# Stage seams, batch-wise row writes, grouped routing and a second accumulator in a two-layer decoder kernel

## What is computed

```python
x = LN(x + spectral(x))                       # fft filter and a bit-correcting code
x = LN(x + gated(x, ctx))                     # two attentions, mixed by a gate
# first ffn: 8 experts, 512 given rows each (rows may repeat)
out_e = gelu(x[tok] @ W1[e] + b1) @ W2[e] + b2
x = LN(x + scatter_add(tok, out_e * combine[tok, e]))
x = LN(x + self_attention(rope(x), 16 heads of 16))
x = LN(x + cross_attention(x, ctx, 16 heads of 64))
# second ffn: 32 experts, top 8 of softmax(x @ gate), capacity 256 rows each
h = silu(x_e @ Wg[e]) * (x_e @ Wu[e])
x = LN(x + scatter_add(slots, (h @ Wdown[e]) * weight))
```

## Time and profile before

| what | us |
| --- | --- |
| median of three runs | 2322.5 |
| lowest and highest | 2320.73, 2326.05 |
| profiled execution | 2315.22 |
| span of its trace | 2313.3 |
| gated to first ffn, no matmul | 380 to 412.9 |
| first ffn to first row maximum of self_heads | 654 to 747.1 |
| cross_heads loop | 1200 to 1936 |
| routing | 1938 to 2050 |
| expert loop, first to last store | 2065.15 to 2283.8 |
| last norm | 2283.8 to 2313.3 |

### The profile page before, as it was taken

The page is one execution under the profiler, slowest core; times in us unless marked ns, Lnnn a source line. Parts: engine busy times, 40 slices in busy tenths (PEclk is TensorE's granted clock), DMA queues, the critical chain, the costliest instruction groups (busy, mean ns, idle before and its releaser), DMA issues. The chain is left out here.

```text
span 2313.3 us, 23934 instructions
## 1 busy us (share of the span) xinstructions
PE 1738.0 (75%) x7497; PEld 1256.8 (54%) x7497; DVE 1236.0 (53%) x2315; ACT 1020.0 (44%) x1920; POOL 1009.3 (44%) x838
## 2 busy tenths in 40 slices
...
DMA packets 88421, 138.38 MB, mean 60 GB/s; under 512 B 19728, under 2 KB 54974, under 8 KB 85480
## 3 DMA queue, kind: packets, MB, share of 16 engines
...
## 5 line engine op out<-in xcount | busy, mean ns | idle before, releaser
L1961 POOL TENSOR_TENSOR STp_lo_use<-ST_use,STp_hi_use 128x512 fp32r<-128x512 f32 x256 | 335.1, 1317 | 163.4 <-ACT ST_use L1812 158.7
L1526 POOL TENSOR_TENSOR STp_lo<-ST,STp_hi 128x512 fp32r<-128x512 f32 x192 | 257.5, 1359 | 117.3 <-ACT ST L1359 116.2
L1808 ACT ACTIVATE STp_hi_use<-bank 128x512 fp32r<-128x512 f32 x256 | 152.8, 597 | 199.2 <-PE bank L1758 196.7
L1355 ACT ACTIVATE STp_hi<-bank 128x512 fp32r<-128x512 f32 x256 | 159.6, 624 | 73.2 <-PE bank L1293 72.6
L1427 DVE TENSOR_REDUCE nmax<-bank 128x1 f32<-128x512 f32 x256 | 168.7, 681 | 34.5 <-PE bank L1282 34.1
L1871 DVE TENSOR_REDUCE nmax_use<-bank 128x1 f32<-128x512 f32 x256 | 170.6, 681 | 5.0 <-PE bank L1732 2.3
L1282 PE MATMUL bank<-rows_k,rows_q 96*128 96x512 f32 x256 | 122.6, 487 | 52.0 <-DVE nmax L1427 44.7
L1359 ACT ACTIVATE ST<-bank 128x512 f32<-128x512 f32 x256 | 161.0, 629 | 0.0
L1812 ACT ACTIVATE ST_use<-bank 128x512 f32<-128x512 f32 x256 | 151.8, 593 | 0.0
L1732 PE MATMUL bank<-ks,qs 128*128 128x512 f32 x256 | 115.9, 454 | 30.3 <-DVE nmax_use L1871 16.2
L2396 POOL DMA_INDIRECT acc_scratch<-res,sidx_all x64 | 101.8, 1591 | 54.9 <-DMA acc_scratch<-res,sidx_all 33.9
...
## 6 DMA issues: line engine op xcount, KB each, us to landing
...
```

What stands on the lines that cost most here:

```text
L1355: A.activation(STp[u % NHI][0], bk.ap, ACT.Exp)
L1526: G.tensor_tensor(STp[u % NHI][1], ST[u % NFULL], plain(STp[u % NHI][0]), ALU.subtract).then_inc(low["pool"].sem, low["pool"].inc(u))
L1808: A.activation(STp[u % NHI][0], bk.ap, ACT.Exp)
L1961: G.tensor_tensor(STp[u % NHI][1], ST[u % NFULL], plain(STp[u % NHI][0]), ALU.subtract).then_inc(low["pool"].sem, low["pool"].inc(u))
```

## The change

- **gated to mixture.** `store(k)` on SP writes the rows of batch k to `rows_scratch` and to the sums while `gated` still works on later batches. The row numbers and combine weights are loaded in `gated`; `tok_row` comes expert by expert (256 KB). The four DMAs of POOL and the two halves are gone.
- **mixture to self_heads.** `norm_sums` is no longer called here. POOL goes on without waiting for its last stores and takes no part in the barrier; the others wait for the stores of the last expert but one. The loads of the sums, statistics, roots and norms are written into `self_heads`: quarter 0 and the statistics of 1 ahead of the step loop, the rest at of_next(s, 38). Zeroing `Vone` moves from DVE to POOL, the zeroing of `rows_q` and `rows_k` goes (one `memset` of one row stays). For batch 0 q0, q1, k0, k1 and the four v results each get a bank of their own. The hop is written by head: 10 DMAs a batch instead of 4, and 4 reads a quarter instead of 9; for batch 0 ACT issues the k half of them.
- **self_heads and cross_heads.** Row tiles have 65 rows instead of 96. In `cross_heads` the takes of the second head move from r = 7 to r = 6 and the output projection and the norm's steps by 2 (one entry by 6).
- **routed.** Rows in `tokens_scratch` are 288 wide, with the 32 weights behind the row, so that a gather brings its weight along. Transposes of a batch run ahead of the logits of the one before; the eight largest are taken batch by batch. The running sum on POOL becomes 15 wide matmuls. BV is made by 16 ACT instructions a group, only for the slots, in f32r with 128 columns. The slot table is written, read back and turned for each group of eight experts, and gathers and stores wait only for their group.
- **two accumulators.** Even experts add into one array, odd ones into another that is filled with zeros by a DMA from DRAM to DRAM; a store waits for the expert before the last. The last norm loads both, and DVE adds them (4 x 128x1024).

```diff
+                if other is not None:
+                    V.wait_ge(others_in[k].sem, others_in[k][k])
+                    V.tensor_tensor(X[:, quarter[k], :], X[:, quarter[k], :], other[:, quarter[k], :], ALU.add).then_inc(added.sem, added.inc(k))
...
+        def store(k):
+
+            tiles = slice(k * TB, (k + 1) * TB)
+            SP.wait_ge(own.sem, own["s2 normed", k])
+            SP.dma_start(kit.rows_d.rearrange("(t p) d -> p t d", p=P)[:, tiles, 0:D], X[:, tiles, :]).then_inc(kit.rows_in.sem, kit.rows_in.inc(k))
+            SP.dma_start(kit.acc_d[0][0:B * S].rearrange("(t p) d -> p t d", p=P)[:, tiles, :], X[:, tiles, :]).then_inc(kit.sums_in.sem, kit.sums_in.inc(k))
+
...
         def pool():
-            G.dma_start(idx, T["idx"]).then_inc(idx_in.sem, idx_in.inc("idx"))
-            G.dma_start(rows_d[:, D:GW], T["combine"]).then_inc(combine_in.sem, combine_in.inc("combine"))
-            G.dma_start(acc_d[0:B * S].rearrange("(t p) d -> p t d", p=P), X).then_inc(acc_in.sem, acc_in.inc("acc"))
-            G.dma_start(tok_row, bass.AP(T["tok"].tensor, 0, [[0, P], [1, E0 * C0]])).then_inc(tok_in.sem, tok_in.inc("tok"))
...
+                SP.dma_start(tok_row[e % 2], bass.AP(T["tok"].tensor, e * C0, [[0, P], [1, C0]])).then_inc(tok_in[e % 2].sem, tok_in[e % 2].inc(e))
...
-        nc.all_engine_barrier()
-    norm_sums(kit, "s3")
+        for engine in (PE, A, V, SP):
+            engine.wait_ge(stored.sem, stored[E0 - 2, CT0 - 1])
+        nc.multi_engine_barrier([PE.engine, A.engine, V.engine, SP.engine])
...
+        def stack_bank(b, n, g):
+
+            return (SPARE, ROW_BANK, *OUT_BANKS)[2 * n + g] if b == 0 else SPARE
+
+        def v_bank(b, t):
+            return (*ST_BANKS, *MAX_BANKS)[t] if b == 0 else SPARE
...
+        def norm_loads(engine, quarters):
+
+            engine.wait_ge(kit.stored0.sem, kit.stored0[E0 - 1, CT0 - 1])
+            for k in quarters:
+                engine.dma_start(X[:, quarter[k], :], tiles_d[:, quarter[k], :]).then_inc(kit.quarter_in[k].sem, kit.quarter_in[k].inc("s3"))
...
+        def stack_rows(engine, b, i, n):
+
+            hs = slice(i * HS, (i + 1) * HS)
+            for k in range(2):
+                first = k * n * HD
+                engine.dma_start(plain((rows_q, rows_k)[n][2 * k * HD:2 * (k + 1) * HD, hs]), hop_d[b % 2, n, hs, first:first + 2 * HD].rearrange("h f s -> f h s")).then_inc(stacked[i].sem, stacked[i].step)
...
-            V.memset(plain(Vone), 0.0).then_inc(own.sem, own.inc("s4 V"))
-            V.wait_ge(own.sem, own["s4 V"])
...
+            average(0)
+            average(1)
+            norm(0)
...
+                if of_next(s, 38) == 0:
+                    norm(1)
+                    average(2)
+                    norm(2)
+                    average(3)
+                    norm(3)
...
-            for rows in (rows_q, rows_k):
-                m = G.memset(plain(rows[MAX_ROW:ROWS]), 0.0)
...
+            G.memset(plain(Vone), 0.0).then_inc(g_own.sem, g_own.inc("s4 V"))
...
-        OUTS = ((50, 0, 0), (58, 0, 1), (STEPS + 18, 1, 0), (STEPS + 24, 1, 1))
+        OUTS = ((50, 0, 0), (58, 0, 1), (STEPS + 24, 1, 0), (STEPS + 25, 1, 1))
...
-                for r, of, half in ((3, "q", 0), (5, "k", 0), (7, "q", 1), (7, "k", 1)):
+                for r, of, half in ((3, "q", 0), (5, "k", 0), (6, "q", 1), (6, "k", 1)):
...
+                def slot_table(g):
+                    PE.wait_ge(slots_in.sem, slots_in[g])
+                    PE.wait_ge(bank[3].free, bank[3].use(("table", g)))
+                    PE.transpose(bank[3].ap[:, 0:16], slot_rows[:, g, :], ident[0:16, 0:16]).then_inc(bank[3].full, 1)
...
                     for t in range(NT):
-                        m = PE.matmul(bank[1 + z].ap[:, 0:256], A_[z][:, t, :, :].rearrange("p e j -> p (e j)"), BV[z][:, t, :, :].rearrange("p v j -> p (v j)"), start=t == 0, stop=t == NT - 1)
+                        m = PE.matmul(bank[1 + z].ap[:, 0:P], A_[z][:, t, :, :].rearrange("p e j -> p (e j)"), BV[z][:, t, :], start=t == 0, stop=t == NT - 1)
...
-                m.then_inc(bank[3].full, 1)
+                    if g:
+                        slot_table(g - 1)
+                slot_table(3)
...
+                for g in range(4):
+                    z = g % 2
+                    A.wait_ge(hot_b.sem, hot_b[g])
+                    if g > 1:
+                        A.wait_ge(bank[1 + z].full, bank[1 + z].full_at["slots", g - 2])
+                    for t in range(NT):
+                        m = A.activation(BV[z][:, t, :], B_[z][:, t, :, :].rearrange("p e j -> p (e j)"), ACT.Copy, scale=token1[:, t:t + 1])
+                    m.then_inc(hot_v.sem, hot_v.inc(g))
...
+                for g in range(4):
+                    e8, z = slice(g * 8, g * 8 + 8), g % 2
+                    if g > 1:
+                        V.wait_ge(bank[1 + z].full, bank[1 + z].full_at["slots", g - 2])
+                        V.wait_ge(hot_v.sem, hot_v[g - 2])
+                    V.tensor_tensor(B_[z], every(lo[:, :, e8], 16), along(ramp[:, 16:32]), ALU.is_equal).then_inc(hot_b.sem, hot_b.inc(g))
+                    V.wait_ge(own.sem, own["high bits"])
+                    V.tensor_tensor(A_[z], every(hi[:, :, e8], 16), along(ramp[:, 0:16]), ALU.is_equal).then_inc(hot_a.sem, hot_a.inc(g))
+                    if g == 0:
+                        weigh()
+                    if g:
+                        agree(g - 1)
+                    if g > 1:
+                        addresses(g - 2)
+                agree(3)
+                addresses(2)
+                addresses(3)
...
-                    G.tensor_tensor(value(z, 0), B_[z], per_tile(token1), ALU.mult).then_inc(hot_v.sem, hot_v.inc(g))
...
-                SP.dma_start(tokens_d.rearrange("(t p) d -> p t d", p=P), X).then_inc(rows_in.sem, rows_in.inc("rows"))
-                SP.dma_start(acc_d[0:B * S].rearrange("(t p) d -> p t d", p=P), X).then_inc(acc_in.sem, acc_in.inc("acc"))
+                SP.dma_start(acc_d[0][0:B * S].rearrange("(t p) d -> p t d", p=P), X).then_inc(acc_in.sem, acc_in.inc("sums"))
+                SP.dma_start(acc_d[1], bass.AP(T["zeros"].tensor, 0, [[0, (B * S + CAP) * D // 4096], [1, 4096]])).then_inc(acc_in.sem, acc_in.inc("zeros"))
+                SP.dma_start(tokens_d[:, 0:D].rearrange("(t p) d -> p t d", p=P), X).then_inc(rows_in.sem, rows_in.inc("rows"))
                 for e in range(WB):
                     load(e)
+                SP.wait_ge(own.sem, own["weight"])
+                SP.dma_start(tokens_d[:, D:].rearrange("(t p) e -> p t e", p=P), weight).then_inc(rows_in.sem, rows_in.inc("weight"))
                 for g in range(4):
                     SP.wait_ge(own.sem, own["slots", g])
-                    for v in range(2):
-                        SP.dma_start(slot_d[v, g * 2048:(g + 1) * 2048].rearrange("(p j) -> p j", j=16), slots[:, g, v, :]).then_inc(slots_out.sem, slots_out.inc((g, v)))
-                SP.wait_ge(slots_out.sem, slots_out[3, 1])
-                SP.dma_start(slot_rows, slot_d.rearrange("v (r c) -> r v c", c=P)).then_inc(slots_in.sem, slots_in.inc("rows"))
+                    SP.dma_start(slot_d[g * 2048:(g + 1) * 2048].rearrange("(p j) -> p j", j=16), slots[:, g, :]).then_inc(slots_out.sem, slots_out.inc(g))
+                    SP.wait_ge(slots_out.sem, slots_out[g])
+                    SP.dma_start(slot_rows[:, g, :], slot_d[g * 2048:(g + 1) * 2048].rearrange("(r c) -> r c", c=P)).then_inc(slots_in.sem, slots_in.inc(g))
...
-                    G.wait_ge(bank[e % 2].full, bank[e % 2].full_at["rows1", e - RB])
+                    bk = bank[6 + (e - RB) % 2]
+                    G.wait_ge(bk.free, bk.free_at["down1", e - RB])
+                if e % 8 == 0:
+                    G.wait_ge(own.sem, own["gidx", e // 8])
                 for t in range(CT1):
...
-            G.wait_ge(own.sem, own["gidx"])
+            G.wait_ge(rows_in.sem, rows_in["weight"])
...
-            G.wait_ge(own.sem, own["sidx"])
+            G.wait_ge(acc_in.sem, acc_in["zeros"])
...
-                if e:
-                    G.wait_ge(stored.sem, stored[e - 1, CT1 - 1])
+                if e % 8 == 0:
+                    G.wait_ge(own.sem, own["sidx", e // 8])
+                if e > 1:
+                    G.wait_ge(stored[e % 2].sem, stored[e % 2][e - 2, CT1 - 1])
...
-                    G.indirect_dma_start(acc_d, bass.IndirectOffsetOnAxis(ap=sidx[:, n:n + 1], axis=0), res[e % 2][:, t, :], None,
-                                         compute_op=ALU.add).then_inc(stored.sem, stored.inc((e, t)))
-            G.wait_ge(stored.sem, stored[E1 - 1, CT1 - 1])
+                    G.indirect_dma_start(acc_d[e % 2], bass.IndirectOffsetOnAxis(ap=sidx[:, n:n + 1], axis=0), res[e % 2][:, t, :], None,
+                                         compute_op=ALU.add).then_inc(stored[e % 2].sem, stored[e % 2].inc((e, t)))
...
-        nc.all_engine_barrier()
-    norm_sums(kit, "s6", kit.out)
```

(1 more changed line is left out.)

454 lines of the change are left out of this document (245 added, 209 removed).

## The result

The changed kernel took **2384.8 us** (median of four runs, 2374.5 to 2393.6) against 2322.5 before: a ratio of **1.027, 95% interval 1.022 to 1.031**. It is slower, by 62 us, where the prediction had it faster by 145. The profiled execution has a span of 2373.2 against 2313.3, 59.9 more.

What follows compares the result with a forecast made beforehand. It took PE to bound dense self_heads and cross_heads, POOL the expert loop, and chains the seams. Terms -24 - 35.6 + 3 - 33 - 35.4 - 22 + 2 = -145 took 2322.5 to 2177 us, range 2138 to 2222.

Steps and rivals of the forecast that it cites:

- Rival (4): self_heads: the new start, PE standing still behind DVE's norms, keeps the granted clock low; 2387 for whole stage, chance 0.03.
- Gated to mixture: Seam from gated's last norm to mixture: gathers start at about 382 instead of 406.19; 24 us gained, range 20 to 26.
- could be late next: Start of mixture: the first expert's weights, 2 MB issued at the same time as the gathers, might be late; nothing priced.
- Mixture to self_heads: Seam from mixture's last store to the first row maximum of self_heads: 35.6 us earlier, range 28 to 40.
- xT: Start of self_heads: the normed, transposed input of the projections is ready at 675.0 instead of 701.66, 26.7 us earlier.
- hop 3, read back 5: Start of self_heads: rows of k go out in 3 us and return in 5, arriving at about 709.
- Inside self_heads: Between first and last row maximum of self_heads: extra hop issues and more pieces at a batch's turn cost 3 us.
- Cross_heads: cross_heads: earlier takes of the second head give 26 us, moved output projections 7; together 33, range 0 to 50.
- An `nmax` wait that takes over from the k wait: cross_heads, a sign of being wrong: PE's wait for maxima grows by what its wait for the second head's k lost.
- Routing: From the end of cross_heads to the first experts of routed: a shorter chain gains 35.4 us, range 26 to 40.
- Expert loop: Expert loop of routed: two accumulators cut the pitch from 6.99 to 6.5, last five experts 5; 22 us gained, range 5 to 31.
- Tail: After the last store: drain and barrier of 5.1 go, but more loads and DVE adds come; 2 us longer.

Runs made afterwards that it cites:

- b_both: Kernel before, with the maximum matmul of self_heads reading 64 rows and the score matmul 65, instead of 96: 2500.7 us, ratio 1.077.
- b_both65: Kernel before, with both the maximum and score matmuls of self_heads reading 65 rows instead of 96: 2323.5 us, ratio 1.001.
- a_pad96: Kernel after, with self_heads row tiles padded by 32 zero rows, so the maximum matmul reads 96 rows and the score matmul 97: 2188.0 us, ratio 0.942.
- a_pad_g: a_pad96 with each head group's hop issued once that group is split, and ACT waiting only for the hop whose place it takes: 2162.7 us, ratio 0.935.

## Why the prediction was wrong

**The step that failed** is one the sum does not even hold: "Row tiles have 65 rows instead of 96" was priced at nothing, without a reason, and the edits of self_heads at +3. No sentence of the prediction weighs the row count. One matmul's length would not have warned: the longest maximum matmul takes 796 ns with 96 rows and 794 with 64. The runs show that the row count changes the clock itself: 177 us between `b_both` and `b_both65`, 197 between the kernel after and `a_pad96`. The change cut rows from 96 to 65 in both matmuls' tiles, but the maximum matmul, which leaves out the row with the maxima, thereby went to 64, on the other side of the edge.

**Rival (4)** gave 2387 with the low clock for the whole stage; 2384.8 came. Its size came out, 196 by the earlier trace rows against 203.8, but by luck: it took the clock for 0.50 throughout, and the stage had 0.62 in the mean; PE was busy for 240 us more, and 36 of them came out of the time in which it had stood still. Its trigger was wrong: it blamed PE's standing still at the new start, and counted for the old clock that "PE stood still just as often there". It got a chance of 0.03, with only that trigger weighed. The trigger that counted stood in the diff.

**Seams.** Gated to mixture: 24 forecast, 17.7 came. The gather came on time, 25.7 earlier; what was mis-sized is the way from there to `GT_hi`, which the prediction left as it was and which took 8.0 us more: 5.1 for the rows to arrive and 2.9 on ACT behind the weights. Of the weights the prediction said that they "could be late next", and priced nothing for them. In the trace after, SP issued them from 385.10 and ACT could take the second half only at 400.95. Mixture itself had no term and grew by 4.9, 4.5 of them in the wait of its last store. Mixture to self_heads: 35.6 forecast, 31.7 came; xT was right within 1.1, and what lacks came behind it. The last half of k was ready sooner than forecast, 9.7 us after the first projection instead of 13, but its rows reached PE 21.0 later, where the prediction had "hop 3, read back 5": the hop's ten issues end only at 696.4. DVE's norms, which the prediction had as late as the rows, were hidden.

**Inside self_heads.** +3 was put for "four hop issues more a batch on SP (0.4 each)". There are six more, 10 instead of 4. They took 0.7 to 1.5 at the medians and up to 1.7, and they do not lie beside the loop: ACT waits for their landing before it takes the next group of the projections. The term is +20 in `a_pad96` and -0.6 in `a_pad_g`.

**Cross_heads.** 26 + 7 forecast, 43.4 came, 39 to 42 of it by the takes alone. PE did stand still for 26 us less, but that the number agrees is partly luck: at the matmul of the forecast the wait fell by 16 (47.1 to 31.1), since the maxima are late there, and 13 came at the first matmul of a step, of which the sum had nothing; others grew. An `nmax` wait that takes over from the k wait was one of the signs of being wrong that the prediction named, and two thirds of it came true. The projections gave next to nothing. What the sum had no line for is again the clock: a PE that waits less was granted 0.98 instead of 0.95, which is worth 16 us of busy time.

**Routing.** 35.4 forecast, 43.4 came: the first expert's transposes are 40.4 earlier (the prediction's own 2050.16 less 2012.5 is 37.7, not 37.4, and it took off 2 for the zero array), and its first store follows them after 12.0 us instead of 15.0. The claim that rows are "long there" when PE reaches the experts is borne out: holding the gather back until the last group costs 7.7, or 16 by the ratios.

**Expert loop.** 22 forecast, 31.1 came. The pitch with a gather is 6.42 against the 6.5 of the prediction; the term that was mis-sized is the last five experts, 3.75 instead of 5, and the 26 times 0.08. Landings with two in flight did not bind: the share rose from 0.71 to 0.78, as worked out, and POOL waited 1.8 us for them in all.

**Tail and the rest.** +2 forecast, +3.7 came. The 8.3 between self_heads and cross_heads are a cost of the low clock for the most part: in `a_pad96` they are 3.9.

Without the clock the sum comes close, 2177 forecast and 2188.0 with 32 zero rows, but because misses cancel. In the traces 126.5 us came of 145. Too much was forecast by some 44: 17 inside self_heads, 10 in the two seams, 15 in stretches that were put at nothing and 2 at the tail. Too little was forecast by some 25: in cross_heads 10, in the routing 6 and in the expert loop 9.
